# Two transformer layers on one core: rotation, key parts and DMA order changed in layer 0; row maxima, projections and value products moved in layer 1

## The reference

```
# layer 0: attention, 32 query heads on 8 key heads, head width 64, window 64
q, k = rms_norm(q), rms_norm(k);  x*cos + rot_half(x)*sin        # rot_half swaps the halves of a head
probs = softmax(q k^T / 8 + sliding mask);  out = (probs v) w_out
# plus a gated FFN of quantised weights (256 -> 704 -> 256) on the same normalised x
# layer 1: attention, 16 heads of width 16, every query sees all 1024 keys
probs = softmax(q k^T / 4);  ctx = probs v;  out = ctx W_out + X
# plus an FFN on the 64 rows of each batch that a router picks, scattered back
```

## Time and profile before

| | us |
|---|---|
| median of 3 runs | 1045.62 (1043.57 to 1057.51) |
| profiled execution | 1048.43 |
| its span | 1046.6 |
| busy in the span: PE, DVE, POOL, ACT | 924.7, 855.2, 705.1, 684.8 |
| layer 1's first reduction (L1343) starts | 684.2 |

### The profile page before, as it was taken

How to read it: one execution, slowest core, us unless ns; L and a number is a source line. 1 busy time by engine, 2 the same in 40 slices (tenths; PEclk the granted TensorE clock), 3 DMA queues, 4 the chain that set the end, 5 groups by cost and what they waited for, 6 DMA issues and landing times. The chain is left out here.

```text
span 1046.6 us, 26415 instructions
## 1 busy us (share of the span) xinstructions
PE 924.7 (88%) x8703; PEld 514.1 (49%) x8703; DVE 855.2 (82%) x1760; ACT 684.8 (65%) x1779; POOL 705.1 (67%) x1034
## 2 busy tenths in 40 slices
PE   3588898998998998998998987788999999999998
PEld 2365665765666666665665665433222222323223
DVE  6797868788888888888788786578999999999871
ACT  2555655655655656565665554217999999898895
POOL 4668878788788888888888878342766765544231
PEclk9698989999999999999999998879999999999999
DMA  5655653454444543444554444243221122222101
GB/s 194 127 115 122 105 95 75 93 106 80 93 97 83 95 99 80 91 98 81 94 98 78 90 86 90 52 131 62 63 38 26 23 42 42 52 40 49 28 1 42
DMA packets 247995, 82.57 MB, mean 79 GB/s; under 512 B 222196, under 2 KB 246452, under 8 KB 247604
## 3 DMA queue, kind: packets, MB, share of 16 engines
q1 hardware_dynamic: 247428, 78.53, 37.5%
q10 hardware_dynamic: 432, 2.36, 0.6%
HBM read 18.49 MB, written 4.19 MB: 22 GB/s over the span
## 5 line engine op out<-in xcount | busy, mean ns | idle before, releaser
L1343 DVE TENSOR_REDUCE l_mxv<-l_mx 128x1 f32<-128x1024 f32 x256 | 294.9, 1214 | 26.2 <-PE l_mx L1545 25.4
L1256 ACT ACTIVATE l_prob<-l_sc 128x512 f32<-128x512 f32 x512 | 273.3, 604 | 17.6 <-PE l_sc L1553 16.5
L427 ACT ACTIVATE an<-an 128x256 f16<-128x256 f32 x128 | 53.3, 416 | 212.8 <-DVE an L601 212.8
L752 POOL TENSOR_TENSOR t<-t 128x320 f32<-128x320 f32 x128 | 110.6, 864 | 114.0 <-DVE t L648 113.9
L1545 PE MATMUL l_mx<-early 48*128 48x512 f16 x512 | 156.3, 387 | 17.7 <-DVE l_mxv L1343 14.5
L743 POOL TENSOR_TENSOR rm<-ss,half_neg 128x5 f32<-128x5 f32 x128 | 156.5, 1223 | 0.0
L1553 PE MATMUL l_sc<-early 50*128 50x512 f16 x512 | 155.7, 382 | 0.3 <-ACT l_prob L1256 0.3
L1516 PE MATMUL l_acc<-l_prob,qkv_all 128*17 128x256 f32 x2048 | 153.9, 384 | 0.0
L881 PE MATMUL qk<-early,xh 128*128 128x384 f16 x512 | 131.2, 339 | 4.4 <-issue 4.0
L934 PE MATMUL ob<-wo_hi,ats 128*128 128x256 f16 x512 | 108.4, 279 | 28.2 <-DMA ats<-an 22.7
L868 PE MATMUL pv<-v,probs 128*64 128x65 f32 x2048 | 90.4, 232 | 29.3 <-ACT probs L476 22.2
(11 more groups left out here) (191 smaller groups left out, 2069.6 us busy)
## 6 DMA issues: line engine op xcount, KB each, us to landing
qkv_all<-w_qkv SPq DMA_DIRECT2D x3, 768.0 KB, 8.5
v<-v SPq DMA_DIRECT2D x64, 32.5 KB, 2.0
xn_all<-xs SPq DMA_DIRECT2D x16, 128.5 KB, 2.1
xa<-x SPq DMA_DIRECT2D x16, 128.0 KB, 2.5
tk<-nat SPq DMA_TRANSPOSE x128, 2.8
qkv_all<-w_o SPq DMA_DIRECT2D x8, 256.0 KB, 3.9
ats<-an SPq DMA_TRANSPOSE x128, 2.5
xc<-x SPq DMA_DIRECT2D x16, 128.0 KB, 2.3
```

The costliest lines, as they stand in the source:

```text
L427: return act.activation(dst, src, ACT.Copy, scale=scale)
L752: pool.tensor_tensor(t1[:, b, :, :], t1[:, b, :, :], t2[:, :, :], ALU.add).then_inc(s_["pool_u"], 1)
L1256: act.activation(prob[:, (y * NI + u) % NPR, h * 512:(h + 1) * 512], sc[:, k % NSC, :], ACT.Exp, scale=D1 ** -0.5).then_inc(s_["act_sc"], 1)
L1343: dve.tensor_reduce(mxv[:, x % 2, u:u + 1], mx[:, MX[k] % 2, :], AX.X, ALU.max).then_inc(s_["dve_mx"], 1)
```

## The change

Layer 0: (a) L647 and L648 become one operation over 640 columns that reads the PSUM tile twice (broadcast) and writes products `tt`; the swap of halves moves into POOL's rotation sum, and the weights of the sine table are laid out to match. (b) The key's low part (L660) moves from near the end of DVE's slot to the front of the next slot, ahead of `rc` (LAG_K = 6). (c) SP issues `tk` in that next slot, ahead of `ats`. (d) ACT's copy of the carried keys into `tk` moves to the front of slot s-7 (LAG_T = 7), the copy back with it to the end of that slot.

Layer 1: (e) `mhl` is padded to 128 columns and turned by a transposing DMA; PE's transpose L1567, ACT's copy and their place in the ring `sc` go away; SP waits for the turned rows before it issues the two row writes. (f) Y and Z tiles stand in the ring `sc` at step 2, in two parts behind the two halves of E; DVE's addition stands ahead of the X reduction of that step. (g) Each piece is split into two parts of two column tiles, and `PIECE_AT` places the parts.

```
-LAG_T = 6
+LAG_K = 6
+LAG_T = 7
...
-                n, k, ok = at(s, LAG_N)
+                n, k, ok = at(s, LAG_K)
...
+                    dve.wait_ge(s_["act_kh"], n * G + k + 1)
+                    dve.tensor_tensor(nat[:, b, 1, 0:HD], t1[:, b, 0, :], nat[:, b, 0, 0:HD], ALU.subtract
+                                      ).then_inc(s_["dve_kl"], 1)
                 n, k, ok = at(s, LAG_V)
...
-                    dve.tensor_tensor(t1[:, b, :, :], heads, tcw[:, i % 2, 0, :, :], ALU.mult)
-                    dve.tensor_tensor(t2[:, :, :].rearrange("p h (a d) -> p h a d", a=2), swapped,
...
+                    dve.tensor_tensor(tt[:, b, :, :, :].rearrange("p j h d -> p j (h d)"),
+                                      qk[:, b, 0:NH * HD].unsqueeze(1).broadcast_to([P, 2, NH * HD]),
...
-                    pool.tensor_tensor(t1[:, b, :, :], t1[:, b, :, :], t2[:, :, :], ALU.add).then_inc(s_["pool_u"], 1)
+                    pool.tensor_tensor(t1[:, b, :, :].rearrange("p h (a d) -> p h a d", a=2),
+                                       t1[:, b, :, :].rearrange("p h (a d) -> p h a d", a=2),
+                                       tt[:, b, 1, :, :].rearrange("p h (a d) -> p h a d", a=2)[:, :, ::-1, :],
...
-PIECE_AT = (7, 9, 9, 11, 13, 15, 17, 19)
+PIECE_AT = ((6, 7), (8, 9), (10, 10), (11, 12), (13, 14), (15, 16), (17, 17), (18, 19))
...
-                pe.wait_ge(s_["act_sc"], SC["E", v, k, 1] + 1)
-                for g in range(4):
+                pe.wait_ge(s_["act_sc"], READ["E", v, k, 1])
+                for g in range(part * 2, part * 2 + 2):
...
+                sp.wait_ge(s_["pool_mh"], t + 1)
+                if t >= 2:
+                    sp.wait_ge(mr_st[t % 2], t // 2 * 32)
+                sp.dma_start_transpose(mrow[:, t % 2, :], mhl[:, t % 2, :]).then_inc(s_["max_turned"], 16)
+                sp.wait_ge(s_["max_turned"], 16 * (t + 1))
+                for j in range(2):
+                    sp.dma_start(qt[row + j:row + j + 1, tile % 4, :],
+                                 mrow[j * NI:(j + 1) * NI, t % 2, :]).then_inc(mr_st[t % 2], 16)
...
+                        if rows_at(c, u) is not None:
+                            rows(rows_at(c, u), h)
+                        for v, k, part in pieces_at(y, u, h):
+                            piece(v, k, part)
```

More of the change, by code:

```diff
@@ L515, in _ @@
                     m = n * G + k
[L516 to L519, removed]
                     landed(act, m)
@@ L997, in pieces_at @@
 def pieces_at(y, u, h):
[L999 to L1002, removed]
+    for k, places in enumerate(PIECE_AT):
+        for part, place in enumerate(places):
+            back, r = divmod(place, 2 * NI)
+            if r == 2 * u + h and 0 <= y - back < ITEMS:
+                yield y - back, k, part
 def place(t):
@@ L1017, in last_of, with rows_at @@
     return tile // 2 * 4 + tile % 2 + 2
-def ahead(c, u):
-    return AHEAD_AT.index((c, u)) if (c, u) in AHEAD_AT else None
+def rows_at(c, u):
+    if (c, u) in AHEAD_AT:
+        return NI + AHEAD_AT.index((c, u))
+    return c - SLOT_Y if u == ROW_AT and 0 <= c - SLOT_Y < NI else None
 def fold_at(c, u):
@@ L1051, in max_units @@
                 order.append(("X", c - LAG_X, u))
[L1052 to L1055, removed]
     return {unit: k for k, unit in enumerate(order)}
 def layer1(nc, loads, spare, idf, idh, ranked, xn2_all, qkv1_all, early, small, front, w_out1, w1, w2, out):
-    SC = score_units()
+    order = score_units()
+    SC = {unit: k for k, unit in enumerate(order)}
+    READ = {unit: sum(o[0] != "Y" for o in order[:k + 1]) for unit, k in SC.items()}
+    MADE = {unit: k + 1 + (unit[0] == "Y") - (order[k - 1][0] == "Y") for unit, k in SC.items()}
     MX = max_units()
@@ L1257, in _ @@
                                            scale=D1 ** -0.5).then_inc(s_["act_sc"], 1)
-                    t = c - LAG_M
-                    if u == 4 and item(t):
-                        k = SC["M", t]
-                        act.wait_ge(s_["pe_sc"], k + 1)
-                        for r in range(2):
-                            wait(act, mr_st[t % 2][r], t // 2 * 16)
-                        ev(mrow[:, t % 2, :], sch[k % NSC][0:2 * NI, 0:P]).then_inc(s_["act_sc"], 1)
                     t = c - LAG_C
@@ L1506, in mod, with free, piece @@
                         ins.then_inc(s_["mod_pe"], 1)
-            def piece(v, k):
-                if k == 0:
+            def free(k):
+                if k >= NSC and order[k - NSC][0] == "Y":
+                    pe.wait_ge(s_["dve_sc"], order[k - NSC][1] + 1)
+                elif k >= NSC:
+                    pe.wait_ge(s_["act_sc"], READ[order[k - NSC]])
+            def piece(v, k, part):
+                if k == part == 0:
                     if v == 0:
@@ L1537, in _ @@
                     if item(y) and u == 0:
-                        for r in range(2):
-                            pe.wait_ge(mr_st[y % 2][r], 16 * (y // 2 + 1))
+                        pe.wait_ge(mr_st[y % 2], 32 * (y // 2 + 1))
                     for h in range(2):
@@ L1573, in _ @@
                         pe.wait_ge(s_["act_acc"], t + 1)
-                        wait(pe, s_["act_sc"], k + 1 - NSC)
+                        free(k)
                         for j in range(2):
```

176 lines of the change are left out of this document (80 added, 96 removed).

## The result

| | us |
|---|---|
| changed kernel, median of 5 runs | 1153.46 (1149.07 to 1162.55) |
| kernel before, median of 5 runs | 1048.32 (1043.57 to 1057.51) |
| ratio | 1.099, 95% interval 1.092 to 1.105 |
| profiled execution, its span | 1162.55, 1160.8 |
| layer 1's first reduction (L1361) starts | 669.4 (before 684.2) |

In the profiled execution layer 0 gained 14.8 us and layer 1 lost 129.0. Against the earlier trace rows, the stretches of the changed kernel: length, busy time of PE, PEld, DVE, ACT, POOL, granted clock, DMA share, GB/s. They are a stretch of layer 0, slot 5, slot 6, slots 8 to 24 and slots 25 to 32.

What follows compares the result with a forecast made beforehand. Before, DVE and PE were both close to full; after, PE was to set layer 1's slot. 1048.4 + 104 (layer 1) - 15 (layer 0) = 1137, less 2.8 for the profiled run: 1134 us, 8-in-10 range 1090 to 1156, own range 1104 to 1155.

Steps and rivals of the forecast that it cites:

- Split products (g): Layer 1: half a product occupies PE as long as a whole one, half-step 0.85 us; slots 8 to 24 +54.4 us.
- The slot's sum, 12.75: Layer 1: PE's work in a plain slot, 12.75 us, exceeds DVE's 9.14, so PE sets the slot.
- the 0.6 us that PE was said to have to spare: Layer 1 before the change: PE's steps sum to 8.9 of a slot's 9.52 us, leaving 0.6 us spare.
- Projections (f): Layer 1: a Y tile adds 1.32 us, slot 14.07; slots 25 to 32 +27.4, 33 to 36 +12.4, 37 and 38 +8.3.
- Row maxima (e): Layer 1: the new path of 7, perhaps 11 us is hidden under a 12.75 us slot; PE loses 0.15 us of work.
- Low part moved (b): Layer 0, DVE: ranking fills its wait for POOL, 0.27 us shorter in some ten of sixteen slots; up to 0.3 lost with norms.
- SP's order (c): Layer 0: `ats` issued up to 1.5 us sooner; `tk` in the same slot or 0.5 us later, about 1 us in hand.
- merged rotation (a): Layer 0: one operation for two saves DVE 0.05 us a slot; POOL's reversed read costs 0.03 more.
- ACT's copy (d): Layer 0: two ACT copies moved within idle time, worth nothing.
- halves at half the price: Rival, layer 1: split products cost half of the passes, 0.12 us; slot 11.4, time 1093 us; chance 0.07.
- hidden: Rival, layer 1: halves and their changes hide wholly on PE, DVE's 9.14 us sets the slot; 1015 us; chance 0.08.
- the power operation that was to hold up the low part: Rival, layer 0: low part waits out any POOL operation, the power too; +0.1 us a slot, 1162 us; chance 0.07.

Runs made afterwards that it cites:

- e9: Layer 0 of the changed kernel, layer 1 of the kernel before with one whole value product in each of the eight steps; 1031.1 us, ratio 0.988.
- e1: The changed kernel with whole value products again at their old places, all else staying changed; 1037.1 us, ratio 0.991 to the kernel before.
- e12: The changed kernel with the first half of product 0 moved from half-step 6 to the empty half-step 5; 1143.1 us, ratio 1.092 to the kernel before.
- e3: Layer 0 of the changed kernel with layer 1 of the kernel before; 1037.0 us, ratio 0.992 to the kernel before.
- e4: The changed kernel with each part of a value product computing all four column tiles, so every product is done twice; 1185.5 us, ratio 1.135 to before.
- e10: The changed kernel, both layers, with whole value products, one in each of the eight steps; 1037.4 us, ratio 0.989 to the kernel before.
- e6: The kernel before with only the merged rotation operation and POOL's reversed read; 1042.9 us, ratio 0.996.
- e8: Layer 0 of the changed kernel, layer 1 of the kernel before with the fold F moved from step 4 to step 3; 1035.8 us, ratio 0.987.

## Why the prediction was right, and where its sums were off

The direction, the mechanism (half a product costs PE what a whole one does, and PE becomes the bound) and most of the size came out: 1134 us forecast, 1153.5 measured, within 1090 to 1156 but near its upper end and just inside the forecast's own 1155. What was missed is a wait in every plain slot.

- **Split products (g)** decide, as forecast: a pass costs the same with two tiles as with four. The forecast took 0.23 for a half product and 0.31 at each end, 0.85 a half-step; measured 0.865. Over the slot that is 12 x 0.015, 0.2 us. That E to product takes 0.09 more than E to X holds in every kernel here, and a product in a step of its own costs 0.2 us more than one behind another (e9). What the 0.09 is made of, the engine emptying or the next weights being loaded, no run separates.
- **The slot's sum, 12.75, was too low** by 0.60, in 17 slots 10 us of the 20 by which the time was missed. 0.2 is in the half-steps; 0.40 is a wait that the sum had no term for. I took PE, once it was the bound, to wait for nothing, and added up its work over the slot. But step 2 is empty: PE is through it in 0.45 us, and then both maxima buffers are full, one of them just being read for 1.22 us. Even an engine that sets the pace waits where its work is uneven and its buffers are two. The trace of before has the same wait in the same step, 0.74 us where 0.22 would do (the lines ahead of e9's). The prediction did not read these lines: most of the 0.6 us that PE was said to have to spare, 0.5, is this wait. It would also be why e1 did not reach DVE's 9.14, which no run shows by itself. e12 shows the wait in the changed kernel by taking it away.
- **Projections (f)**: forecast +1.32 a Y slot over the plain one, measured 14.33 - 12.95 = 1.38; slots 25 to 32 +29.6 against 27.4, slots 33 to 36 +12.6 against 12.4, slots 37 and 38 +7.7 against 8.3. The forecast's whole Y slot, 14.07, was too low by those 0.06 and the half-steps' 0.2. DVE's addition lay under PE's time, as forecast: no wait of PE for it stands in slots 8 to 32. Under whole products a Y slot of e1 is 0.28 us longer than one of e3, and there E's weight loads wait for that addition, 5.1 us in eight slots.
- **Row maxima (e)**: hidden, as forecast; no wait of PE or ACT for them stands among those of slots 8 to 32. The 0.15 us that PE was to save were wrong: in the earlier trace rows the transpose stands between product and F, and a pair of products up to what follows takes 0.99 us even without it (e4), 834.44 + 0.99 = 835.43 against F's start at 835.47. So e1's slot is 0.03 shorter, not 0.15; between e9 and e10 it is 0.10.
- **Low part moved (b), SP's order (c), merged rotation (a), ACT's copy (d)**: layer 0 gained 14.8 us where -15 was taken. That the two agree is luck: -15 was a choice between -40 and +10 and no sum, and e3's median shows 9.3 us of it. The low part fell to 0.38 us; (a) saved 0.06 a slot against 0.05; POOL's reversed read took 864 ns on average, as L752 in the earlier trace rows, where 0.03 was allowed. Wrong was the sentence that `tk` lands with about 1 us in hand: 18 waits of 15.4 us in all say otherwise. Of these 9 (7.6 us) follow POOL's low part of the queries, 5 (3.0 us) the moved low part and 4 (4.8 us) neither.
- **Slots 5 and 6** were not in the sum. In the profiled execution they cost 11 us at the lower clock; in e1 and e12 they cost nothing. The other runs of the changed kernel have a mean clock of 0.976 to 0.982 against 0.968, so less of the median than of the profiled run is this. The sum for layer 1 without them is 118 against 104 forecast.
- **Rivals**: halves at half the price, or hidden, are excluded by e4 and by the timeline; the power operation that was to hold up the low part did not: from 200 to 640 us of the changed kernel, the 17 low parts that ran beside it took 0.20 us.

## What to carry to other kernels

Splitting work to fill gaps on PE pays only if the part is cheaper than the whole: compare the spacing of starts, and count the changes between kinds of matmul, not the matmuls. When an engine becomes the bound, its time is its sum plus the waits that uneven steps and a short ring still force on it; look for the step that is nearly empty. A wait taken from one place in a chain of near-equal engines shows up as another one, so ask who is next before undoing the change that it appeared with.

## What the runs showed of the hardware

- Four fp32 matmuls in two of the four column tiles keep PE for 0.54 us up to the next X, eight in all four tiles for 0.56: an empty tile saves next to nothing.
- In the changed kernel the key's low part, with two SBUF inputs, takes 0.42 us on average where it starts beside POOL's L756 (52 times from 200 to 640 us) and 0.46 beside L766 (17 times), but 0.20 beside POOL's power operation L747 (17 times), though all three read SBUF.
- Reading the halves of a head reversed costs POOL nothing: 863 ns on average over 128 instructions in e3, 864 in the kernel before.
- The same slots 5 and 6 took 29.1 us in e1, at a granted clock of 0.68 and then 1.00, and 41.5 to 41.6 in the profiled runs of the changed kernel, e6, e8 and e10, at 0.51 to 0.52 and then 0.57 to 0.58. That is 12 us. Both e1 and the changed kernel had PE half idle before (4.19 and 4.13 of 10 us busy); what decides which clock follows stays open.
